# Two-layer transformer on one core: narrower causal-mask matmuls in the attention stage, router gates carried inside the dispatched rows, and a last stage that adds two rows

## The chip, the cores and the metric

The kernel runs on one core of one Trainium2 chip, as one program. The metric is the device time of one execution in microseconds (us), the median over the runs shown. Engines are named as in the profile: PE is the matmul engine (PEld its weight loads), DVE the vector engine, ACT the scalar engine, POOL the GpSimd engine, SP the engine that issues most DMAs.

## What is computed

The input is x[32, 256, 128] in float32: 32 batches of 256 tokens with 128 channels, 8192 tokens in all. Two layers follow each other, each an attention part and a mixture-of-experts part, both modulated per batch (`mod`). What matters here:

```
layer 0 attention (8 heads of 16):
  scores = (rope(q) . rope(k)) / 4;  scores = where(causal, scores, -inf)
  out    = softmax(scores) v, mixed with a second ("geometric") causal softmax; x = x + ga * out Wo
layer 0 experts (32, top 4); layer 1 attention (a delta rule over 256 steps), output projection
layer 1 experts (8, top 2):
  scores = rmsnorm(h) router;  ids = top2(scores);  c = softmax(scores)[ids]
  y_e    = W_down[e] (val * silu(gate)),  [val, gate] = W_up[e] rmsnorm(h)
  out    = sum over the 2 ids of c * y_id, plus h;  x = x + gb * out
```

## The kernel before

The kernel is a row of phases, each closed by a barrier over all engines: setup, load, attention, route, experts, project, delta, mix, ffn, combine. Inside a phase every engine has its own hand-written program, and they meet through semaphores. The change touches four phases; the order of the work in each is written out by hand.

**Attention** (`attention_phase`, from L467) loops over 32 batches, and over 2 groups of 4 heads in each. `scores` (L556 to L571) makes the scores of a group, for 8 blocks of 32 queries; a block's keys lie side by side in one of three PSUM banks (`KEYS_AT`: blocks 6 and 7 have 256 columns each in bank 0, blocks 4 and 5 have 192 and blocks 0 and 1 have 64 in bank 1, blocks 2 and 3 have 128 in bank 2). For each pair of blocks a bfloat16 matmul of the identity with a mask table (L565) first writes the causal term (-1e30 or 0) over all columns of both blocks; then one float32 product per block (L569, two records each in the profile) adds q.k on top. DVE reads the maxima bank by bank (`read_max`, L713), ACT makes the exponentials (L632), DVE transposes them (L725), and PE multiplies by the values (`weigh`, L581). PE's order in a batch is: scores of group 0, q and k of the next batch, scores of group 1, `front_geo`, weigh group 0, mix, weigh group 1, v of the next batch.

**Mix** (`mix_phase`, from L2236) goes through the tokens in 8 rounds of 1024. In each, the layer-1 attention output is projected, normalised and modulated, and the router picks 2 experts per token. DVE's `choose` finds them, `rank` gives each its place (L2696), ACT's `exps` makes exponentials (L2528), and DVE's `share` (L2700 to L2702) turns them into the two gates, written to the table `g.gate1`. POOL's `send` waits for the places, copies them (L2781), and issues 16 indirect DMAs (L2792), each of which scatters 128 rows of 132 floats (128 channels, then the row's destination number in column 128, then padding) to the area of the chosen expert; it then writes the next round's numbers (L2778). DVE's order in an iteration b is roots(b), choose(b-1), ..., rank(b-1), in the last one `tile_table` (L2710 to L2723), share(b-1), statistics, skip. In iteration b=1 choose and rank stand ahead of `scale_heads` (L2614), share behind it.

**Ffn** (`ffn_phase`, from L2801) takes 136 tiles of 128 rows: SP loads a tile (`xg`), PE multiplies with the expert's weights, DVE copies the result out of PSUM (L2942), and POOL scatters the rows by their number to `choice_rows`.

**Combine** (`combine_phase`, from L2955) goes through 16 chunks of 512 tokens, two to an iteration. SP loads the two rows of each token (two DMAs of 256 KB to a chunk, L2979, buffers for two chunks), DVE multiplies each by its gate (L3019) and adds them (L3025), PE transposes to channels (L2988), DVE applies the modulation and adds the kept x (L3031), PE transposes back (L2994), ACT copies out of PSUM (L3004) and issues the store (L3008). SP may load into a buffer again when its products have been taken.

## Time and profile before

| what | us |
|---|---|
| median of 3 runs (2347.59 to 2360.34) | 2350.3 |
| the profiled execution | 2352.5 |
| its span, first to last instruction | 2350.7 |
| PE / DVE / ACT / POOL busy | 1886.6 / 1631.3 / 1337.8 / 1241.9 |
| mean granted clock of PE | 0.869 of full speed |

The profile is one execution, so durations are those of that execution; 1.8 us lie outside its span. Share of busy time is an average over ten phases with different limits, so each phase is read by itself below.

### The profile page before, as it was taken

Reading aid. Unit: us, or ns where it says so; the run is one execution under the profiler, and the core shown is the slowest. Engines: PE = TensorE matmul, PEld = TensorE weight load, DVE = VectorE, ACT = ScalarE, POOL = GpSimd, SP = SyncE. Lnnn points to the kernel's source line nnn. Section 1 sums busy time; section 2 is a strip of 40 time slices with the busy share of each in tenths; the row PEclk is TensorE's granted clock in tenths of the full one; section 3 lists DMA queues with packets and bytes.
Section 4 is the critical chain, followed back from the end, with each engine's and each line's share of the span. In section 5 each row is a group of like instructions: output and inputs, shape, how many; then the busy total and the mean of one; then the engine's idle time right before and its main releaser. Section 6 shows DMA issues by size and latency. Waiting matters only on the chain. (4 is left out here: it accounts for less than half of the span.)

```text
span 2350.7 us, 38590 instructions
## 1 busy us (share of the span) xinstructions
PE 1886.6 (80%) x10634; PEld 1503.8 (64%) x10666; DVE 1631.3 (69%) x5209; ACT 1337.8 (57%) x3237; POOL 1241.9 (53%) x1241
## 2 busy tenths in 40 slices
PE   4689999999996663858996799999876641999975
PEld 3577777777774442325664688888765531999973
DVE  5678888888886695427996888888555442555547
ACT  3566666666663597316774688888444331555541
POOL 2177777777773000762324588888824454444430
PEclk8699999999998675978998899999876555999995
DMA  3000000000002112333200000000030011222217
GB/s 108 20 1 1 1 1 1 1 1 1 1 1 113 57 35 61 48 49 111 81 19 1 1 1 1 1 1 1 25 149 30 33 41 54 70 66 65 65 55 200
DMA packets 103522, 92.36 MB, mean 39 GB/s; under 512 B 11728, under 2 KB 93776, under 8 KB 102608
## 3 DMA queue, kind: packets, MB, share of 16 engines
q1 hardware_dynamic: 80272, 63.39, 8.7%
q0 software_dynamic: 14592, 22.30, 3.6%
q10 hardware_dynamic: 8448, 4.20, 0.6%
q8 instruction: 91, 1.49, 0.3%
q14 instruction: 119, 0.97, 0.1%
HBM read 46.87 MB, written 42.98 MB: 38 GB/s over the span
## 5 line engine op out<-in xcount | busy, mean ns | idle before, releaser
L581 PE MATMUL attn_out<-attn_turned,attn_v_diag 128*128 128x512 f32 (+7 forms) x1024 | 266.7, 414 | 22.4 <-DVE attn_turned L725 20.2
L618 ACT ACTIVATE attn_p_geo<-attn_kp_wide,attn_geo_cols 128x32 f32<-128x32 f32 (+6 forms) x448 | 179.6, 495 | 165.7 <-DVE attn_geo_cols L705 165.7
L581 PEld LDWEIGHTS attn_out<-attn_turned,attn_v_diag 128*128 128x128 f32 x1024 | 178.1, 191 | 122.3 <-issue 89.8
L2835 POOL DMA_INDIRECT choice_rows<-ffn_y,ffn_xg x136 | 130.9, 963 | 170.8 <-DVE ffn_y L2942 165.4
L2221 POOL TENSOR_TENSOR delta_A<-delta_A,delta_sW 128x256 f32<-128x256 f32 x256 | 186.9, 730 | 58.7 <-ACT delta_sW L2085 21.0
L569 PE MATMUL attn_score<-attn_k,attn_q_diag 128*128 128x256 f32 (+3 forms) x1024 | 183.5, 316 | 2.1 <-POOL attn_q_diag L797 0.5
L632 ACT ACTIVATE attn_p_att<-attn_score,attn_mx 128x224 f32<-128x224 f32 (+7 forms) x512 | 148.8, 390 | 62.4 <-DVE attn_mx L713 62.4
L2085 ACT ACTIVATE delta_sW<-delta_W,tables_sb 128x256 f32<-128x256 f32 x256 | 129.0, 506 | 79.2 <-DVE delta_W L2180 76.3
L569 PEld LDWEIGHTS attn_score<-attn_k,attn_q_diag 128*128 128x128 f32 x1024 | 157.5, 192 | 16.3
L2011 PE MATMUL delta_u<-delta_m,tables_sb 128*128 128x256 f32 x512 | 161.2, 397 | 3.6 <-DVE delta_m L2158 3.6
L2007 PE MATMUL delta_u<-delta_v_own,tables_sb 128*128 128x256 f32 x512 | 153.6, 382 | 8.7 <-DVE xnT L2145 8.7
L2019 PEld LDWEIGHTS delta_out<-delta_m,tables_sb 128*128 128x128 f32 x1024 | 131.9, 194 | 44.7 <-POOL delta_m L2232 40.9
L2019 PE MATMUL delta_out<-delta_m,tables_sb 128*128 128x128 f32 x1024 | 142.5, 283 | 19.9 <-POOL delta_m L2232 19.9
L2232 POOL TENSOR_TENSOR delta_m<-delta_A,delta_prod 128x1024 f32<-128x1024 f32 x64 | 151.4, 2365 | 5.0
L2792 POOL DMA_INDIRECT rows<-mix_rows,mix_slot x128 | 125.1, 978 | 44.9 <-issue 38.9
L2167 DVE TENSOR_TENSOR delta_u<-delta_u,delta_prod 128x256 f32<-128x256 f32 x256 | 110.8, 433 | 50.7 <-PE delta_u L2011 27.0
L713 DVE TENSOR_REDUCE attn_mx<-attn_score 128x2 f32<-128x512 f32 (+3 forms) x256 | 109.5, 478 | 43.4 <-PE attn_score L569 43.4
L1281 POOL DMA_INDIRECT exp_rows<-rows,slot_token x32 | 33.2, 1039 | 201.3 <-POOLq L136 191.8
L2180 DVE TENSOR_TENSOR delta_W<-delta_W,delta_u 128x128 f32<-128x128 f32 x512 | 133.7, 282 | 4.5
L797 POOL TENSOR_TENSOR attn_q_diag<-attn_q,tables_sb 128x1024 f32<-128x1024 f32 x64 | 120.4, 1905 | 0.0
L2934 DVE TENSOR_TENSOR ffn_hid<-ffn_sg,ffn_val 128x384 f32<-128x384 f32 x136 | 75.3, 554 | 61.6 <-PE ffn_val L2858 51.1
L725 DVE STREAM_TRANSPOSE attn_turned<-attn_p_att 128x32 f32<-128x32 f32 (+7 forms) x512 | 112.9, 288 | 2.7 <-ACT attn_p_att L632 2.7
(400 smaller groups left out, 5100.1 us busy)
## 6 DMA issues: line engine op xcount, KB each, us to landing
ffn_xg<-rows SPq DMA_DIRECT2D x136, 66.0 KB
acc<-route_zero SPq DMA_DIRECT2D x10, 832.0 KB
comb_rows<-choice_rows SPq DMA_DIRECT2D x32, 256.0 KB
rows<-route_rows SPq DMA_DIRECT2D x8, 640.0 KB, 3.5
load_rows<-in_x SPq DMA_DIRECT2D x16, 256.0 KB
bT<-acc SPq DMA_DIRECT2D x16, 256.0 KB, 3.9
qT<-acc SPq DMA_DIRECT2D x16, 256.0 KB, 4.6
x_kept<-xT SPq DMA_DIRECT2D x16, 256.0 KB, 2.1
```

The lines of the kernel that those rows point to most:

```text
L569: last = nc.tensor.matmul(score[bank][:, c:c + size], q_diag[:, gr, n], kk[:, par, 0:size], start=False, stop=n == here[-1])
L581: last = nc.tensor.matmul(out[:, :, SLOT * n:T], v_diag[:, gr, n], turned[:, :, gr, n * T + SLOT * n:(n + 1) * T], start=n == 0, stop=n == ...
L618: nc.scalar.activation(p_geo[:, gr, EARLY_OFF[n]:EARLY_OFF[n + 1]], kp_wide[:, par, gr, 0:n, :].rearrange("p n i -> p (n i)"), ACT.Exp, sc ...
L632: last = nc.scalar.activation(p_att[:, gr, ROW_OFF[n]:ROW_OFF[n + 1]], score[at][:, c:c + SLOT * (n + 1)], ACT.Exp, bias=mx[:, gr, n:n + 1])
L2007: nc.tensor.matmul(corrections(h, pp % 2), g.t("same_head"), moving, start=True, stop=False)
L2011: nc.tensor.matmul(corrections(h, pp % 2), g.t("same_head"), m1[:, h].rearrange("p t d b -> p (t d b)"), start=False, stop=True).then_inc( ...
L2019: last = nc.tensor.matmul(out_ps[parity][:, 0:QUAD * B], g.t(f"give{d}"), m3[:, parity, :, d, :], start=d == 0, stop=d == DH1 - 1)
L2085: nc.scalar.activation(sW[:, step % RING, :], W[:, step % RING].rearrange("p d b -> p (d b)"), ACT.Copy, scale=g.t("step")[:, bass.ds(step ...
L2180: nc.vector.tensor_tensor(W[:, t % RING, :, some(h)], W[:, (t - 1) % RING, :, some(h)], changes(h, pp % 2)[:, n], ALU.subtract).then_inc(b ...
L2221: nc.gpsimd.tensor_tensor(A[:, t % 8], A[:, (t - 1) % 8], sW[:, t % RING], ALU.add).then_inc(k.A, 1)
L2232: nc.gpsimd.tensor_tensor(m3[:, t // QUAD % 2], sums, query, ALU.mult).then_inc(k.m3, 1)
L2835: nc.gpsimd.indirect_dma_start(g.choice_rows, bass.IndirectOffsetOnAxis(xg[:, n % RING, D:D + 1].bitcast(U32), 0), y[:, n % RING, :], None ...
```

## The change

1. Attention: the mask matmul covers only the last 64 columns of each block, 128 columns in all, in place of 512, 384, 256 and 128. For blocks 4 and 6 (`TRIMMED`) the q.k product is cut to the 160 and 224 columns that a query of the block can see.
2. Gates: `share` writes the two gates of a token to column 129 of the rows to be sent. POOL's `send` therefore waits for the end of the round's route chain (`c.route`) before its first DMA. In iteration b=1 ACT's `exps` moves ahead of `add_bias` and `modulate`, and DVE's `share` ahead of `scale_heads`. In ffn, DVE's copy out of PSUM becomes a multiplication by the gate that came with the row.
3. Combine: the multiplications are gone; loads are four chunks deep, each chunk is a step of its own, and PE and DVE interleave chunk c with chunk c-1.

```diff
@@ -85,8 +85,8 @@
-    own, none = np.where(late, NEG, 0.0), np.zeros((128, T))
-    b["mask_pair"] = np.concatenate([none[:, 2 * SLOT:], own, none[:, SLOT:], own[:, 0:SLOT]], axis=1)
+    own, none = np.where(late, NEG, 0.0), np.zeros((128, SLOT))
+    b["mask_pair"] = np.concatenate([own, none, own[:, 0:SLOT]], axis=1)
...
+TRIMMED = (4, 6)
...
@@ -562,12 +563,14 @@
                     for n in here[1::2]:
                         _, c, size = KEYS_AT[n]
                         pair = score[bank][:, c - size:c + size].rearrange("p (n j) -> p n j", n=2)
-                        nc.tensor.matmul(pair, g.t("ident_bf"), g.t("mask_pair").rearrange("p (n j) -> p n j", n=2)[:, :, T - size:T],
-                                         start=n == here[1], stop=False)
+                        nc.tensor.matmul(pair[:, :, size - 2 * SLOT:size], g.t("ident_bf"),
+                                         g.t("mask_pair").rearrange("p (n j) -> p n j", n=2),
+                                         start=n == here[1], stop=False, skip_group_check=True)
                     for n in here:
                         _, c, size = KEYS_AT[n]
-                        last = nc.tensor.matmul(score[bank][:, c:c + size], q_diag[:, gr, n], kk[:, par, 0:size],
-                                                start=False, stop=n == here[-1])
+                        seen = SLOT * (n + 1) if n in TRIMMED else size
+                        last = nc.tensor.matmul(score[bank][:, c:c + seen], q_diag[:, gr, n], kk[:, par, 0:seen],
+                                                start=False, stop=n == here[-1], skip_group_check=True)
...
                 if b >= 1:
                     copy_rows(b - 1, 0)
+                if b == 1:
+                    exps(b - 1)
                 for par in both:
...
                 if b >= 1:
                     copy_rows(b - 1, 1)
+                if b > 1:
                     exps(b - 1)
...
@@ -2699,8 +2704,10 @@
                 dve.wait_ge(c.exp, i + 1)
...
-                then(nc.vector.tensor_tensor(g.gate1[:, tiles(i), :], ex[:, :, E1:E1 + K1], total[:, :, None].to_broadcast([128, SIDE, K1]),
-                                             ALU.mult))
+                shares = rows[:, i % 2, :, :, :, D + 1].rearrange("p a j n -> p (a j) n")
+                if i == 0:
+                    dve.wait_ge(c.ids_made, 3)
+                then(nc.vector.tensor_tensor(shares, ex[:, :, E1:E1 + K1], total[:, :, None].to_broadcast([128, SIDE, K1]), ALU.mult))
...
                 if b == 1:
                     then = choose(b - 1)
                     rank(b - 1)
+                    share(b - 1, then)
...
                 if b == LAST + 1:
                     tile_table()
-                if b >= 1:
+                if b > 1:
                     share(b - 1, then)
...
-            nc.gpsimd.memset(rows[:, :, :, :, :, D + 1:ROW1].rearrange("p a b j n w -> p (a b j n) w"), 0.0).then_inc(c.ids_made, 1)
+            nc.gpsimd.memset(rows[:, :, :, :, :, D + 2:ROW1].rearrange("p a b j n w -> p (a b j n) w"), 0.0).then_inc(c.ids_made, 1)
...
                 pool.wait_ge(c.named, i + 1)
                 pool.wait_ge(c.slots, i + 1)
+                pool.wait_ge(c.route, ROUTE * (i + 1))
                 for par in both:
                     pool.wait_ge(k[par].rows_read, i + 1)
...
                 dve.wait_ge(k[par].down, n // 2 + 1)
                 if n >= RING:
                     dve.wait_ge(ring[n % RING].sent, 16 * (n // RING))
-                nc.vector.tensor_copy(y[:, n % RING, :], y_ps[par][:, 0:D]).then_inc(k[par].y, 1)
+                nc.vector.tensor_scalar(y[:, n % RING, :], y_ps[par][:, 0:D], xg[:, n % RING, D + 1:D + 2], None, ALU.mult)\
+                    .then_inc(k[par].y, 1)
...
+    DEEP = 4
     with Scope(nc, "comb") as s:
-        rows = s.sb("rows", [128, PAR, K1, TILES, D])
-        part = s.sb("part", [128, PAR, K1, TILES, D])
-        mixed = s.sb("mixed", [128, PAR, TILES, D])
...
+            for c in range(NCH):
+                if c >= DEEP:
+                    sp.wait_ge(k.mixed, c - DEEP + 1)
+                for n in range(K1):
+                    sp.dma_start(rows[:, c % DEEP, n], by_tile(g.choice_rows[chunk(c, n * N), :])).then_inc(rows_in[c % DEEP], 16)
...
+            def turn(c):
+                pe.wait_ge(k.mixed, c + 1)
+                if c > 1:
+                    pe.wait_ge(k.y, c - 1)
+                for r in range(TILES):
+                    last = nc.tensor.transpose(by_channel[c % 2][:, 128 * r:128 * r + 128], mixed[:, c % 2, r, :], g.t("ident"))
+                last.then_inc(k.turned, 1)
+
+            def back(c):
+                pe.wait_ge(k.y, c + 1)
+                if c > 1:
+                    pe.wait_ge(k.copied, c - 1)
+                for r in range(TILES):
+                    last = nc.tensor.transpose(by_row[c % 2][:, 128 * r:128 * r + 128], y[:, c % 2, 128 * r:128 * r + 128],
+                                               g.t("ident"))
+                last.then_inc(k.back, 1)
+
+            for c in range(NCH + 1):
+                if c < NCH:
+                    turn(c)
+                if c > 0:
+                    back(c - 1)
...
+            def add(c):
+                dve.wait_ge(rows_in[c % DEEP], 32 * (c // DEEP + 1))
+                if c > 1:
+                    dve.wait_ge(k.turned, c - 1)
+                nc.vector.tensor_tensor(mixed[:, c % 2], rows[:, c % DEEP, 0], rows[:, c % DEEP, 1], ALU.add).then_inc(k.mixed, 1)
...
+            def gate(c):
+                dve.wait_ge(k.turned, c + 1)
...
+            for c in range(NCH + 1):
+                if c < NCH:
+                    add(c)
+                if c > 0:
+                    gate(c - 1)
...
-        g.gate1 = ctx.enter_context(nc.sbuf_tensor("gate1", tiles, F32))
```

## Rows read from the trace of the kernel before

**Rows 1.** timeline of one attention batch: start us, duration us, engine, line, what

```profile
409.38 4.18 PE L581 MATMUL attn_out<-attn_turned,attn_v_diag 128*128 128x512 f32 x16 [0.66 <-DVE attn_turned L725]
...
415.16 0.69 DVE L713 TENSOR_REDUCE attn_mx<-attn_score 128x2 f32<-128x512 f32 x1 [0.78 <-PE attn_score L569]
...
416.48 1.09 DVE L713 TENSOR_REDUCE attn_mx<-attn_score 128x2 f32<-128x384 f32 x3 [0.62 <-PE attn_score L569]
...
417.26 1.58 ACT L632 ACTIVATE attn_p_att<-attn_score,attn_mx 128x160 f32<-128x160 f32 x6 [0.46 <-DVE attn_mx L713]
```

**Rows 2.** page, part 5: busy us, mean ns, then idle us before

```profile
L713 DVE TENSOR_REDUCE attn_mx<-attn_score 128x2 f32<-128x512 f32 (+3 forms) x256 | 109.5, 478 | 43.4 <-PE attn_score L569 43.4
...
L725 DVE STREAM_TRANSPOSE attn_turned<-attn_p_att 128x32 f32<-128x32 f32 (+7 forms) x512 | 112.9, 288 | 2.7 <-ACT attn_p_att L632 2.7
```

**Rows 3.** timeline of POOL in mix: rounds 1 and 6, and the last round

```profile
1781.53 0.98 POOL L2792 DMA_INDIRECT rows<-mix_rows,mix_slot  x1 [0.77 <-POOL mix_slot L2781]
...
1801.80 0.22 POOL L2778 COPY mix_rows<-mix_ids 128x16 uint32<-128x16 uint32 x1
...
1932.42 0.98 POOL L2792 DMA_INDIRECT rows<-mix_rows,mix_slot  x1 [0.77 <-POOL mix_slot L2781]
...
1957.22 0.98 POOL L2792 DMA_INDIRECT rows<-mix_rows,mix_slot  x1 [0.77 <-POOL mix_slot L2781]
1960.40 1.79 POOL L2792 DMA_INDIRECT rows<-mix_rows,mix_slot  x1 [2.19 <-issue]
...
1978.93 0.96 POOL L2792 DMA_INDIRECT rows<-mix_rows,mix_slot  x1 [0.30 <-issue]
```

**Rows 4.** timeline of DVE over the same rounds, and ffn's first instruction

```profile
1782.82 0.20 DVE L2702 TENSOR_TENSOR gate<-mix_ex,mix_total 128x16 f32<-128x16 f32 x1
...
1804.41 1.29 DVE L2614 TENSOR_TENSOR mix_on<-mix_mid,xnT 128x512 f32<-128x512 f32 x2 [13.95 <-remote]
...
1934.55 0.18 DVE L2702 TENSOR_TENSOR gate<-mix_ex,mix_total 128x16 f32<-128x16 f32 x1
...
1963.53 0.17 DVE L2702 TENSOR_TENSOR gate<-mix_ex,mix_total 128x16 f32<-128x16 f32 x1
...
1984.22 0.27 DVE L2919 MEMSET ffn_w_up<- 128x256 f32 x1 [20.51 <-PEq L136]
```

**Rows 5.** stretches in us: busy us of each engine, PE's clock, DMA share, GB/s

```profile
2005.00:2275.00 270.00, 270.00 (x2423) 270.00 (x2422) 150.86 (x382) 159.56 (x380) 123.13 (x128) 1.00 0.23 63
2288.00:2340.00 52.00, 26.86 (x112) 20.37 (x112) 38.86 (x72) 7.99 (x14) 0.00 (x0) 0.53 0.79 222
2300.00:2306.00 6.00, 3.86 (x16) 3.00 (x16) 4.90 (x10) 0.60 (x1) 0.00 (x0) 0.50 0.93 259
2340.00:2350.70 10.70, 3.94 (x16) 3.01 (x16) 4.67 (x9) 1.57 (x3) 0.00 (x0) 0.50 0.32 99
```

**Rows 6.** timeline of PE on the mask and score products, group 1 of a batch

```profile
399.45 0.38 PE L565 MATMUL attn_score<-tables_bf_sb 128*128 128x512 bf16 x1
...
399.66 1.03 PE L569 MATMUL attn_score<-attn_k,attn_q_diag 128*128 128x256 f32 x4
...
400.53 0.38 PE L565 MATMUL attn_score<-tables_bf_sb 128*128 128x384 bf16 x2
...
400.74 1.26 PE L569 MATMUL attn_score<-attn_k,attn_q_diag 128*128 128x192 f32 x8
...
401.84 0.27 PE L565 MATMUL attn_score<-tables_bf_sb 128*128 128x256 bf16 x1
```

**Rows 7.** timeline of the end of combine

```profile
2341.66 1.29 DVE L3025 TENSOR_TENSOR comb_mixed<-comb_part 128x512 f32<-128x512 f32 x2
...
2342.40 1.97 PE L2988 MATMUL comb_by_channel<-tables_sb,comb_mixed 128*128 128x128 f32 x8 [2.66 <-DVE comb_mixed L3025]
2343.55 1.73 DVE L3031 SCALAR_TENSOR_TENSOR comb_y<-comb_by_channel,mod,xT 128x256 f32<-128x256 f32 x4 [0.61 <-PE comb_by_channel L2988]
...
2346.49 0.60 ACT L3004 ACTIVATE comb_done<-comb_by_row 128x512 f32<-128x512 f32 x1 [0.26 <-PE comb_by_row L2994]
```

More of the change, by code:

```diff
@@ L2569, in _ @@
             dve.wait_ge(c.consts, 5)
-            tiles = lambda i: bass.ds(i * SIDE, SIDE)
             def roots(run, heads, norm, rms):
@@ L2955, in combine_phase @@
 def combine_phase(nc, dram, g, out):
+    DEEP = 4
     with Scope(nc, "comb") as s:
-        rows = s.sb("rows", [128, PAR, K1, TILES, D])
-        part = s.sb("part", [128, PAR, K1, TILES, D])
-        mixed = s.sb("mixed", [128, PAR, TILES, D])
-        y = s.sb("y", [128, PAR, CH])
-        done = s.sb("done", [128, PAR, TILES, D])
-        by_channel = [s.ps(f"by_channel{par}") for par in range(PAR)]
-        by_row = [s.ps(f"by_row{par}") for par in range(PAR)]
-        k = [s.sems("in0 in1 part0 part1 mixed turned y back copied out", par) for par in range(PAR)]
+        rows = s.sb("rows", [128, DEEP, K1, TILES, D])
+        mixed = s.sb("mixed", [128, 2, TILES, D])
+        y = s.sb("y", [128, 2, CH])
+        done = s.sb("done", [128, DEEP, TILES, D])
+        by_channel = [s.ps(f"by_channel{n}") for n in range(2)]
+        by_row = [s.ps(f"by_row{n}") for n in range(2)]
+        k = s.sems("mixed turned y back copied")
+        rows_in = list(s.sems("in0 in1 in2 in3").values())
+        sent = list(s.sems("out0 out1 out2 out3").values())
         block = s.block()
         out_rows = out.rearrange("b t c -> (b t) c")
-        cols = lambda i, par, first=0: bass.ds(i * (PAR * CH) + par * CH + first, CH)
-        both = range(PAR)
+        chunk = lambda c, first=0: bass.ds(first + c * CH, CH)
         by_tile = lambda ap: ap.rearrange("(r p) c -> p r c", p=128)
@@ L2998, in _ @@
         @block.scalar
         def _(act):
-            for i in range(0, NCH // PAR):
-                for par in both:
-                    act.wait_ge(k[par].back, i + 1)
-                    act.wait_ge(k[par].out, 16 * i)
-                    nc.scalar.activation(done[:, par].rearrange("p r c -> p (r c)"), by_row[par][:, :], ACT.Copy)\
-                        .then_inc(k[par].copied, 1)
-                for par in both:
-                    act.wait_ge(k[par].copied, i + 1)
-                    act.dma_start(by_tile(out_rows[cols(i, par), :]), done[:, par]).then_inc(k[par].out, 16)
@@ L3009, in _ @@
-            for par in both:
-                act.wait_ge(k[par].out, 16 * (NCH // PAR))
+            for c in range(NCH):
+                act.wait_ge(k.back, c + 1)
+                if c >= DEEP:
+                    act.wait_ge(sent[c % DEEP], 16 * (c // DEEP))
+                nc.scalar.activation(done[:, c % DEEP].rearrange("p r c -> p (r c)"), by_row[c % 2][:, :], ACT.Copy).then_inc(k.copied, 1)
+                act.wait_ge(k.copied, c + 1)
+                act.dma_start(by_tile(out_rows[chunk(c), :]), done[:, c % DEEP]).then_inc(sent[c % DEEP], 16)
@@ L3012, in _ @@
+            for n in range(DEEP):
+                act.wait_ge(sent[n], 16 * (NCH // DEEP))
         @block.vector
         def _(dve):
-            for i in range(0, NCH // PAR):
-                for c in range(K1):
-                    for par in both:
-                        dve.wait_ge((k[par].in0, k[par].in1)[c], 16 * (i + 1))
-                        share = g.gate1[:, bass.ds(i * (PAR * TILES) + par * TILES, TILES), c:c + 1]
-                        nc.vector.tensor_tensor(part[:, par, c], rows[:, par, c], share.to_broadcast([128, TILES, D]), ALU.mult)\
-                            .then_inc((k[par].part0, k[par].part1)[c], 1)
-                for par in both:
-                    dve.wait_ge(k[par].part0, i + 1)
-                    dve.wait_ge(k[par].part1, i + 1)
-                    dve.wait_ge(k[par].turned, i)
-                    nc.vector.tensor_tensor(mixed[:, par], part[:, par, 0], part[:, par, 1], ALU.add).then_inc(k[par].mixed, 1)
-                for par in both:
-                    dve.wait_ge(k[par].turned, i + 1)
-                    dve.wait_ge(k[par].back, i)
-                    for j in range(BPC):
-                        b = i * (PAR * BPC) + par * BPC + j
-                        last = nc.vector.scalar_tensor_tensor(y[:, par, j * T:(j + 1) * T], by_channel[par][:, j * T:(j + 1) * T],
-                                                              g.mod[:, 1, 5, bass.ds(b, 1)], g.keptT[:, bass.ds(b * T, T)],
-                                                              ALU.mult, ALU.add)
-                    last.then_inc(k[par].y, 1)
@@ new lines, in add @@
+            def add(c):
[5 more added lines that the diff above has]
+                dve.wait_ge(k.turned, c + 1)
+                if c > 1:
+                    dve.wait_ge(k.back, c - 1)
+                for j in range(BPC):
+                    b = c * BPC + j
+                    last = nc.vector.scalar_tensor_tensor(y[:, c % 2, j * T:(j + 1) * T], by_channel[c % 2][:, j * T:(j + 1) * T],
+                                                          g.mod[:, 1, 5, bass.ds(b, 1)], g.keptT[:, bass.ds(b * T, T)],
+                                                          ALU.mult, ALU.add)
+                last.then_inc(k.y, 1)
@@ L3120, in build @@
         g.keptT = g.xT
-        tiles = (128, N // 128, K1)
-        g.gate1 = ctx.enter_context(nc.sbuf_tensor("gate1", tiles, F32))
         g.w_up = ctx.enter_context(nc.sbuf_tensor("w_up_sb", [128, E1 * 2, HID], F32))
```

20 lines of the change are left out of this document (removed).

## The prediction

> **What bounds the kernel now.** I read the page first: ten phases with different limits, so the 80% of PE says little, and the change touches four of them. Then came the stretches by phase, the timeline inside each, and the groups with their idle time.
>
> *Attention* is a loop through two engines. PE starts to weigh group 1 only when DVE has transposed it (idle 0.66 us), then makes v and the next batch's first scores; DVE meanwhile waits, 0.78 us for bank 0 and 0.62 us for bank 1 [rows 1]. Over all batches DVE waits 43.4 us for scores, 1.4 in each, while before the transposes it waits 2.7 us in all [rows 2]: behind the second bank DVE runs nearly dense round to the next weighing. So what PE saves between weighing and bank 1 of group 0 shortens the loop; what it saves in group 1 falls into its 0.66 us of idleness.
>
> *Mix* is set, unexpectedly, by POOL's sends. Round 1 issues its 16 from 1781.53 to 1801.80; DVE, which wants only a PE product for L2614, stands still 13.95 us and goes on at 1804.41 [rows 3, 4], 2.6 us behind the last send, though the trace puts that product's matmuls several us earlier. In all seven rounds that have a successor something in this chain resumes 2.5 to 2.9 us behind the last send. The page has no name for it ("remote"); I take it that PE's results are held up while the sends run. A later send is then a later round.
>
> *Ffn* is PE alone: 270.00 of 270 us busy [rows 5]. *Combine* waits for loads: with two chunks of buffers, a load starts when products are done. DMA engines are busy 0.79 of 2288 to 2340, 0.93 in a good stretch, 0.32 in the tail [rows 5].
>
> **Attention: the change on PE.** A float32 product of 256 columns takes 0.87 / 4 = 0.22 us per record, two passes of 0.107. One of 192 columns takes 0.163, so the four records of 64 columns in the row of eight take (1.10 - 0.65) / 4 = 0.11, not the 0.054 of their columns: 0.11 is the floor that the weight load sets [rows 6]. The 512-column mask takes 0.21; cut to 128 columns it would take 0.053, but the float32 weights behind it need 0.107, so bank 0 saves 0.107, and 2 x 0.027 for block 6 with 224 columns: 0.16. In bank 1 the 384-column mask falls from 0.16 to 0.053, since only another mask's light load follows; with 2 x 0.027 for block 4 that is 0.16 again. The masks of 256 and 128 columns already lie at or under the floor: nothing. On the path: 0.32 us in each of 31 later batches, **-9.9 us**. The same 0.32 in group 1 is hidden by PE's idleness. Next in line is ACT, with 0.46 us of idleness before its exponentials of banks 1 and 2 [rows 1]; 0.32 fits. The bounds are 0 (another wait takes over) and, if the floor did not hold, -12.
>
> Here a rule can be set against the row. The Trainium skill (TensorE: Matmul & The Clock Gate, Back-to-back issue gap) gives an isolated matmul a gap of its columns alone, and warns that this under-counts at few columns. By the columns alone bank 0 would save 0.21 and bank 1 0.16, 0.37 us a batch, 11.6 us in all. The records of 64 columns side with the warning, and the sum stays at 9.9.
>
> **Mix: the added wait.** POOL now waits for the gates before the first send; queued behind that wait are the 16 sends and the next round's numbers, and the next round, or ffn, waits for those. Between sends POOL idles 0.30 us [rows 3], so I take the first send 0.3 behind the gates' end. In round 1: 1782.82 + 0.20 + 0.3 = 1783.3 against 1781.53, 1.8 later. In round 6: 1934.73 + 0.3 against 1932.42, 2.6 later [rows 3, 4]. In the four between, the gates are ready between just before and 1.5 us after the first send; the six sum to 7.9. Round 0 has its exponentials and gates moved forward, with ACT's table load ahead of them; I put its send 0.6 us later. In the last round the tile table stands ahead of the gates: 1963.70 + 0.3 = 1964.0 against 1957.22, 6.8 later. But those 16 sends took until 1979.89, 22.7 us against the 20.3 of round 1, with a 2.19 us hole while DVE made the table [rows 3]; behind the table that hole closes, leaving about 4.0, and ffn's start moves with it [rows 4]. Sum if every delay counts: 0.6 + 7.9 + 4.0 = **+12.5 us**. The lower bound is +4, where only the last round counts; the upper +17, if the POOL launch takes the 0.77 us that it takes behind its own copy and round 0 loses the full 1.5 us by which its DVE work shifts. I take the sum, since every round resumes behind the sends.
>
> **Ffn and the rest.** DVE's copy becomes a multiplication by a per-row value over the same 128 x 128; there is no row for that form, so between the copy's own time and twice it. The cover is PE: DVE is busy 150.86 of 270 us [rows 5], and even 0.3 us more on each of 136 tiles leaves it below 200. Nothing. If the cover were gone, 41 us would lie open. The smaller mask table and the narrower memset lie in starts that wait for other work: nothing.
>
> **Combine.** The whole DMA work is 0.79 x 52 + 0.32 x 10.7 = 44.5 us at full share [rows 5]. Four chunks deep, loads need not wait for DVE: a chunk costs 2.8 us of DMA, while DVE needs 0.65 + 0.87 and PE 1.97 [rows 7]. SP issues two loads a chunk and ACT one store, all short against 2.8. The last three stores (2.8 us) still come behind the last load. At a share of 0.97, midway between the best stretch and 1, loads end at 2289 + 41.7 / 0.97 = 2332.0. The tail is an addition 0.65, transposes 1.0, modulation 0.9, transposes 1.0, four hand-overs of 0.1, and 4.2 from the last copy to the end (2346.49 to 2350.7): 8.2 [rows 7]. End 2340.2, **-10.5 us**. Bounds: -5.6 (share 0.93, no store left behind) and -12.
>
> **Sum.** -9.9 + 12.5 - 10.5 = -7.9. Against the profiled execution's 2352.5 that gives 2344.6; the median of the runs is 2.2 lower, so the forecast is 2342.4, 0.3% less than before. About 0.5%, 11.8 us, is what a measurement of this kernel can tell from no change.
>
> **Rivals.**
> - *The delays in mix are absorbed.* If what holds PE up ends by itself, or more of PE's chain slips through before the later sends, only the last round counts, +4. Against it: the constant 2.5 to 2.9 us. For it: the delay is 2 us in rounds of 25 to 36, and POOL has pauses. -9.9 + 4 - 10.5 = -16.4: 2333.9. Chance 0.27.
> - *Combine stays tied to DMA.* More loads and stores in flight may only lengthen each; share at 0.93 and no store left behind: -5.6 in place of -10.5, 2347.3. Chance 0.10.
> - *Narrow masks bring nothing*: the mask stays covered by the weight load or by ACT and POOL, whose slack is 0.46 us and less. Then the first part doesn't do what it says; 2352.3. Chance 0.09.
> - *Slower: fewer links slip through under the sends.* In rounds 5 and 6, 25 us long where rounds 1 to 4 have 32, only the count and the places are left behind the sends. If the later start costs these two that progress, each grows by 7: +14, 2356.3. It decides once the first matmul of `widen` is no longer done before the hold-up sets in; if rounds 1 to 4 also fall to the 36 us of round 0, up to 16 more. Chance 0.12.
>
> **Numbers.** The forecast has 0.42. 2330 to 2357 holds all but the far ends of the first rival (a floorless -12 in attention) and the heavy form of the last. Faster by over 0.5% (below 2338.5) is the absorbed case and a tail of the forecast, where combine and attention reach their far bounds: 0.36. Slower by over 0.5% is the heavy form of the last: 0.07. The rest, 0.57, is no change.
>
> **What would show it.** Right: DVE's idle time before L713 falls by about 10 us, attention by the same; sends begin 0.3 us behind the gates, rounds 1 and 6 start their successors 1.8 and 2.6 us later, ffn's first instruction stands at about 1984.2 - 9.9 + 12.5 = 1986.8; ffn lasts as long as before; combine takes some 52 us at a DMA share near 0.9. Wrong: a round that starts on time although its sends were late; a POOL launch that takes much more than 0.3 us behind the gates; PE idle in ffn with DVE as its releaser; DVE's wait for bank 1 gone, with ACT or POOL as the new releaser.

## The result, and the profile after

The changed kernel took 2325.49 us (median of 4 runs, 2325.06 to 2329.91) beside 2350.05 for the kernel before: a ratio of 0.9897, 95% interval 0.9877 to 0.9917, 24.6 us less. The forecast was 2342.4, in a range from 2330 to 2357. The profiled execution took 2325.7 us, with a span of 2323.9, which is 26.8 less than before. The trace gives the length of each stage, from its first instruction to that of the next:

| us | setup, load | attention | route | experts | project | delta | mix | ffn | combine |
|---|---|---|---|---|---|---|---|---|---|
| before | 109.9 | 634.8 | 187.8 | 120.4 | 223.4 | 421.4 | 285.7 | 303.6 | 62.9 |
| after | 111.1 | 625.5 | 183.7 | 126.2 | 224.5 | 421.5 | 283.0 | 303.1 | 44.5 |
| difference | +1.2 | -9.3 | -4.1 | +5.8 | +1.1 | +0.1 | -2.7 | -0.5 | -18.4 |
| forecast | 0 | -9.9 | 0 | 0 | 0 | 0 | +12.5 | 0 | -10.5 |

Route and experts, which the change leaves alone, come out at 183 to 184 or 188 to 193, and at 120 to 126, from run to run; their +1.7 together is no effect. So attention came as forecast, mix was 15.2 us better than forecast and combine 7.9.

**Attention.** The page of after, part 5 (busy us, mean ns, then idle us before; compare [rows 2]):

```profile
L716 DVE TENSOR_REDUCE attn_mx<-attn_score 128x2 f32<-128x512 f32 (+3 forms) x256 | 109.5, 478 | 33.6 <-PE attn_score L572 33.6
...
L728 DVE STREAM_TRANSPOSE attn_turned<-attn_p_att 128x32 f32<-128x32 f32 (+7 forms) x512 | 113.0, 289 | 2.7 <-ACT attn_p_att L635 2.7
```

DVE waits 9.8 us less for scores (43.4 before), the releaser is still PE, and the wait before the transposes, which would have grown if ACT had become the next limit, has stayed at 2.7. The timeline of PE over one group's scores (start, duration; compare [rows 6]):

```profile
396.32 0.22 PE L566 MATMUL attn_score<-tables_bf_sb 128*128 128x128 bf16 x1
396.38 1.03 PE L572 MATMUL attn_score<-attn_k,attn_q_diag 128*128 128x224 f32 x4
397.25 0.28 PE L566 MATMUL attn_score<-tables_bf_sb 128*128 128x128 bf16 x2
397.36 1.21 PE L572 MATMUL attn_score<-attn_k,attn_q_diag 128*128 128x160 f32 x8
```

From the mask of bank 0 to the first mask of bank 1 it is 0.93 us where it was 1.08, and from there to the mask of bank 2 (which starts at 398.40) 1.15 where it was 1.31: 0.15 and 0.16 less, as worked out.

**Mix.** The timeline of DVE and POOL in round 6 and where the last round begins (start, duration, idle before; compare [rows 3, 4]):

```profile
1926.25 0.23 DVE L2692 TENSOR_TENSOR mix_place<-mix_small,mix_base 128x64 f32<-128x64 f32 x1 [14.06 <-DMA exp_rows<-rows,slot_token]
...
1927.60 0.19 DVE L2710 TENSOR_TENSOR mix_rows<-mix_ex,mix_total 128x16 f32<-128x16 f32 x1
...
1944.02 0.19 DVE L2710 TENSOR_TENSOR mix_rows<-mix_ex,mix_total 128x16 f32<-128x16 f32 x1
```

```profile
1928.64 0.98 POOL L2801 DMA_INDIRECT rows<-mix_rows,mix_slot  x1 [1.18 <-issue]
...
1948.04 0.96 POOL L2801 DMA_INDIRECT rows<-mix_rows,mix_slot  x1 [0.30 <-issue]
...
1950.10 0.98 POOL L2801 DMA_INDIRECT rows<-mix_rows,mix_slot  x1 [0.77 <-issue]
```

Round 6 sends 0.85 us behind the end of its gates (1928.64 less 1927.79), not 0.3. The last round's gates stand ready at 1944.2, tile table included, while POOL is busy with the set of sends before until 1949.0: the new wait holds nothing there. Counted from the start of the stage, the first send of rounds 0 to 7 stands at

| | 0 | 1 | 2 | 3 | 4 | 5 | 6 | 7 | last send ends |
|---|---|---|---|---|---|---|---|---|---|
| before | 47.3 | 83.0 | 114.9 | 147.0 | 178.5 | 209.0 | 233.9 | 258.7 | 281.4 |
| after | 48.8 | 86.7 | 117.1 | 150.4 | 179.1 | 210.1 | 235.3 | 256.8 | 278.6 |

Rounds 0 and 1 are late by 1.5 and 3.7, more than I had priced (0.6 and 2.4); then the delay doesn't add up: it is 2.2, 3.4, 0.6, 1.1 and 1.4, and the last set starts 1.9 early.

**Combine.** Stretches of after (busy us of PE, PEld, DVE, ACT, POOL; PE's clock, DMA share, GB/s; compare [rows 5]):

```profile
2285.00:2291.00 6.00, 4.63 (x22) 3.88 (x22) 4.44 (x9) 1.19 (x2) 0.00 (x0) 0.51 1.17 292
2291.00:2297.00 6.00, 4.11 (x28) 2.68 (x27) 4.44 (x9) 1.79 (x3) 0.00 (x0) 1.00 1.16 328
...
2303.00:2309.00 6.00, 4.58 (x22) 3.40 (x20) 4.24 (x9) 1.79 (x3) 0.00 (x0) 0.58 1.15 345
...
2315.00:2323.90 8.90, 3.00 (x20) 1.81 (x18) 2.77 (x7) 1.79 (x3) 0.00 (x0) 0.87 0.54 167
```

The DMA engines are at 1.15 to 1.17, above the 1 that I took for a ceiling. The share adds up the time of packets, so a share above 1 says that packets of one engine overlapped. The packet work over the seven stretches from 2279 (four are shown; the shares of the six full ones add up to 6.52) is 6 x 6.52 + 8.9 x 0.54 = 43.9 us, close to the 44.5 of the forecast; it is done in less time.

### The profile page after: what moved, and what is told of

Same layout as the page of the kernel before. It is cut to its first block and busy times, and to the rows that moved or that the text cites. A ratio compares the mean times of both kernels' runs of the same rounds, so it can differ in the third digit from the quotient of the medians.

```text
span 2323.9 us, 38564 instructions
## 1 busy us (share of the span) xinstructions
PE 1881.0 (81%) x10666; PEld 1491.0 (64%) x10666; DVE 1618.6 (70%) x5177; ACT 1337.9 (58%) x3237; POOL 1241.1 (53%) x1241
## 5 line engine op out<-in xcount | busy, mean ns | idle before, releaser
L584 PE MATMUL attn_out<-attn_turned,attn_v_diag 128*128 128x512 f32 (+7 forms) x1024 | 268.8, 416 | 24.9 <-DVE attn_turned L728 21.4
L572 PE MATMUL attn_score<-attn_k,attn_q_diag 128*128 128x64 f32 (+5 forms) x1024 | 177.8, 317 | 0.0
L572 PEld LDWEIGHTS attn_score<-attn_k,attn_q_diag 128*128 128x128 f32 x1024 | 149.5, 193 | 7.3
L1284 POOL DMA_INDIRECT exp_rows<-rows,slot_token x32 | 33.6, 1049 | 197.5 <-POOLq L136 188.0
L716 DVE TENSOR_REDUCE attn_mx<-attn_score 128x2 f32<-128x512 f32 (+3 forms) x256 | 109.5, 478 | 33.6 <-PE attn_score L572 33.6
L800 POOL TENSOR_TENSOR attn_q_diag<-attn_q,tables_sb 128x1024 f32<-128x1024 f32 x64 | 120.4, 1903 | 0.2 <-PE attn_score L572 0.2
```

Of the source, the lines that this page charges most:

```text
L572: last = nc.tensor.matmul(score[bank][:, c:c + seen], q_diag[:, gr, n], kk[:, par, 0:seen], start=False, stop=n == here[-1], skip_group_ch ...
L584: last = nc.tensor.matmul(out[:, :, SLOT * n:T], v_diag[:, gr, n], turned[:, :, gr, n * T + SLOT * n:(n + 1) * T], start=n == 0, stop=n == ...
```

## The experiments

Times of different chips can't be compared (the kernel before took 2350 and 2347 us on two and 2300 to 2302 on four others), so every ratio is against the kernel before on the same chip, and stage lengths come from each run's own trace. The gap between those chips lies in mix. On the first two it lasts 275 to 291 us, because other engines stand still for long stretches while POOL sends ("the hold-up" below); on the other four it lasts 227 to 232. Of the kernel before, only one trace shows a chip with the hold-up, the one that the prediction was read from.

**One part at a time.** Four kernels, each the one before with one part of the change, on a chip without the hold-up. The edits are shown shortened.

The mask products and the trimmed columns:

```diff
-nc.tensor.matmul(pair, ..."mask_pair"...[:, :, T - size:T], ...)
+nc.tensor.matmul(pair[:, :, size - 2 * SLOT:size], ..."mask_pair"..., ...)
+seen = SLOT * (n + 1) if n in TRIMMED else size
```

> The kernel before with the attention part of the change alone (narrow masks, products of blocks 4 and 6 cut). Theory 'floor' (the step of the prediction): PE saves 0.32 us on the path in each of 31 batches, so the attention stage falls from 634.8 to about 625 us and the whole by 9.9 us (0.42%). Rival 'columns': 0.37 us a batch, 11.6 us. Rival 'nothing': another wait takes over, within 2 us of before. The mix stage has the same code as before (285.7 us); how far it moves here is what it moves by itself.

Measured: ratio 0.9949 (0.9931 to 0.9967), attention 624.9 us where the other kernels on this chip have 634.6 to 635.4, DVE's wait for scores 33.6. The ratio alone can't tell 9.9 us from 11.6; the stage and the wait side with 9.9. The price by the weight load's floor stands, and nothing else took over.

The wait, and round 0's exponentials and gates moved forward, the gates still in their table:

```diff
+pool.wait_ge(c.route, ROUTE * (i + 1))
...
+if b == 1: exps(b - 1)
...
+    share(b - 1, then)
```

> The kernel before with POOL's added wait for the gates and the forward move in round 0, gates still written to their table; nothing else. Theory 'held' (the prediction's): every round ends as much later as its sends begin later; with sends 0.86 us behind the gates, as in the changed kernel, that is about 12.5 + 4 = 16 us, mix 302 us, whole +0.7%. Rival 'absorbed': only the last round's sends count, +3 to +4 us, mix 289 us, whole +0.15%. Rival 'free': the rounds have other limits and the mix stage stays within 3 us of 285.7, as it does in the changed kernel (283.0).

Measured: ratio 0.9993 (0.9978 to 1.0008). But this chip has no hold-up: mix lasts 229.1, its rounds are POOL's own 21.4 us, and from round 2 on the gates are ready 4 to 15 us before POOL sends. Free here says nothing of the other kind of chip.

Combine four chunks deep with the multiplications kept, and the reverse, no multiplications (the gates in the rows, as in the change) in the old two-chunk combine:

```diff
-rows = s.sb("rows", [128, PAR, K1, TILES, D])
+rows = s.sb("rows", [128, DEEP, K1, TILES, D])
```

> The kernel before with the four-deep, chunk-by-chunk combine of the change, multiplications kept on DVE, gates in their table. Combine before: 62.9 us, in the changed kernel 44.5. If depth is what gave the 18.4 us: DVE then has 3 x 0.69 + 0.87 = 2.9 us a chunk, 47 us for 16, more than the DMA at 345 GB/s (2.3 us a chunk), so about 47 + 4 + 5 = 56 us, whole -7 us. If loads were limited to the share of 1.0 that the prediction took, no difference to that can be seen, since DVE is slower. If the multiplications never mattered: 45 us, -18 us.

```diff
-nc.vector.tensor_tensor(part[:, par, c], rows[:, par, c], share..., ALU.mult)   # 4 x an iteration
-nc.vector.tensor_tensor(mixed[:, par], part[:, par, 0], part[:, par, 1], ALU.add)
+nc.vector.tensor_tensor(mixed[:, par], rows[:, par, 0], rows[:, par, 1], ALU.add)
```

> The kernel before with the gates in the rows (mix and ffn as changed) and a combine of the old two-chunk structure whose multiplications are gone, a buffer being free once the addition is done. If the multiplications were on the loop of load and product: each of 8 iterations loses 2 x 0.65 us at least, combine about 62.9 - 10 = 52 us. If depth is everything: combine within 3 us of 62.9. Mix and ffn: theory 'held' wants mix at 302 us, 'absorbed' 289, 'free' 283 to 288; ffn stays at 303.5 in every theory.

Measured: combine 53.6 us, ratio 0.9959 (0.9942 to 0.9976), and 51.0 us, ratio 0.9953 (0.9933 to 0.9973). Against the 63 to 65 that combine takes as it was, depth with the chunk-by-chunk order gives some 10 and the missing products some 12.5; both together give 18.4, so some 4 are counted twice. Ffn with the multiplication in the copy's place took 304.4 us, within its spread (303.1 to 304.7).

**On a chip with the hold-up**: the changed kernel once more, the wait alone once more, and two other depths.

```diff
-DEEP = 4
+DEEP = 2   # f_deep2; DEEP sets the buffers of the loads and of the stores
+DEEP = 8   # f_deep8
```

> The changed kernel, measured again beside the parts. Additive theory: mask part -11.7, deep chunk-wise combine without multiplications -18.4, gates in the rows and the added wait 0 where mix runs at POOL's own pace (228 us): about -30 us, ratio 0.987. 'Held' theory: where mix takes 286 us in the kernel before, the added wait costs +12 to +16 and the ratio is 0.992 to 0.995.

> The kernel before with the added wait and the forward move in round 0 alone, once more. If mix takes 286 us in the kernel before on this chip, 'held' says +12 to +16 us, 'absorbed' +3 to +4, 'free' within 3. If mix takes 227 us, POOL alone sets the rounds (21.4 us each) and all say 0 to +2: round 0 begins its sends about 1 us behind the gates and nothing else is late.

> The changed kernel with loads two chunks deep in place of four. If depth lifts the DMA rate above what the prediction took as full: a load may start only when the addition two chunks back is done, DMA falls to about 250 GB/s, combine 44.5 to about 52 us, +0.3%. If the chunk-wise order and the shorter DVE work are enough: within 2 us of 44.5.

> The changed kernel with loads eight chunks deep. If combine now runs at the DMA engines' own rate (328 to 345 GB/s in its middle), no more depth helps: within 1 us of 44.5. If the rate still grows with what is in flight, combine falls by 2 to 4 us.

| | ratio (95%) | mix | combine |
|---|---|---|---|
| changed kernel | 0.9882 (0.9848 to 0.9917) | 278.5 | 44.9 |
| wait alone | 1.0009 (0.9989 to 1.0030) | 279.6 | 64.5 |
| depth 2 | 0.9898 (0.9874 to 0.9922) | 275.2 | 51.0 |
| depth 8 | 0.9864 (0.9836 to 0.9892) | 290.7 | 45.6 |

The wait alone costs nothing that can be measured, with the hold-up present (+2 us, interval -3 to +7): this is the run that takes my 12.5 us away. The wait was at work in it: in its trace the first sends of rounds 0 to 6 each stand 0.8 to 1.0 us behind their gates. Depth 4 is worth 6 us over depth 2, depth 8 no more; and at depth 2 the new order takes the same 51.0 us as the old order without products, so of the 18.4 us some 12 are the products and some 6 the depth, and the order alone gives nothing.

Mix moves from 275 to 291 between kernels that are the same there, so one trace on such a chip can't price a few us of it. In the one of 290.7 the last round's sends came 37.4 us behind those before, in the others 21.4 to 21.5. The timeline of POOL in that trace shows the last round's places taken and then a pause:

```profile
1941.91 0.20 POOL L2789 CAST mix_slot<-mix_place_of 128x16 uint32<-128x16 f32 x1 [8.79 <-DVE mix_place_of L2701]
1950.23 0.98 POOL L2801 DMA_INDIRECT rows<-mix_rows,mix_slot  x1 [8.12 <-issue]
```

DVE made the tile table from 1941.76 on and the gates behind it, until 1949.38. So the cost that I had put on the last round, a wait for gates behind the table, was paid in this one execution: 8.12 us of idle POOL where the launch behind its copies takes 0.77 [rows 3], some 7.3 us. In the four other traces with the wait on such a chip it was not.

**The attention term split**: the masks narrow, all score columns kept.

```diff
 last = nc.tensor.matmul(score[bank][:, c:c + size], ..., kk[:, par, 0:size], ...)
```

> The kernel before with the mask products cut to 128 columns, while the q.k products keep their full 192 and 256 columns. Of the 0.32 us a batch that the two edits gave together, my sum puts 0.107 + 0.107 on the narrow masks (a 512-column and a 384-column mask each fall to the float32 weight load behind them) and 0.054 + 0.054 on the trimmed columns. Theory (weight-load floor, both parts on the loop): attention 634.8 - 31 x 0.214 = 628.2, 6.6 us less, the rest of the 9.9 missing. Rival 1 (the masks pay by their columns and the trimmed columns lie under something): attention at 625, 9.9 us less. Rival 2 (the trimmed columns did most of it): attention at 631 or more.

Measured: ratio 0.9988 (0.9972 to 1.0003), attention 628.1. The page of this kernel, part 5, and below it that of the kernel before on the same chip:

```profile
L714 DVE TENSOR_REDUCE attn_mx<-attn_score 128x2 f32<-128x512 f32 (+3 forms) x256 | 109.4, 477 | 36.9 <-PE attn_score L570 36.9
```

```profile
L713 DVE TENSOR_REDUCE attn_mx<-attn_score 128x2 f32<-128x512 f32 (+3 forms) x256 | 109.4, 477 | 43.5 <-PE attn_score L569 43.5
```

The wait falls by 6.6 us = 31 x 0.214, to the tenth the two savings of 0.107 (one down to the floor, one of 256 columns); the other 3.3 (to 33.6) are the trimmed columns. By the mask's columns alone it would have been 0.16 + 0.107 a batch, 8.3 us. The ratio is little help: 6.6 us would be 0.9971, just outside its interval, and other stages differed from the trace beside it by as much (route by 5.2 us).

**The wait, doubled, and POOL paused.** The question left was why later sends cost nothing. All of these fell on chips without the hold-up (mix of the kernel before beside them 227.8, 227.5 and 231.7). A memset ahead of the first send of each round:

```diff
 pool.wait_ge(c.slots, i + 1)
+nc.gpsimd.memset(idle[:, :], 0.0)      # 128x2112
 for par in both:
```

> The kernel before with a POOL memset of 128x2112 in front of the first send of each round of mix, about 1.86 us each by the one row of that size, 15 us over eight rounds. It doubles the cost that I suspected: every run of sends starts 1.9 us later, with nothing else changed. On a chip with the hold-up (mix 280 to 286): my prediction's rule (a later run of sends is a later round) says mix 13 to 15 us longer; the rival (what is held gets through at other points, and a later run of sends is caught up) says less than 4 us. On a chip without it (mix 227, POOL-bound) both say 15 us longer, mix 242, and the run tells nothing on the rule.

> Again the kernel before with a POOL memset of 128x2112 (1.86 us each) in front of the first send of each round of mix. On a chip without the hold-up (mix 227 us) the first time gave 239.9, 12.4 us more. If this chip has the hold-up (mix about 280): my prediction's rule says mix 13 to 15 us longer than the kernel before beside it; the rival, that the delay is caught up, says less than 4 us. Without the hold-up: 240 again.

Measured: ratio 1.0034 (1.0017 to 1.0051), mix 239.9, 12.4 more for 14.9 us of memsets; then 1.0038 (1.0018 to 1.0057), mix 238.4, 6.7 more than the single trace beside it, which was itself 4 us longer than elsewhere. The ratios, over ten executions each, say 8 and 9 us more (4 to 13). Where POOL is the bound, some half or more of what is put on POOL is paid. On the rule, neither run tells anything.

A pause of 0.55 us after the first eight sends of a round:

```diff
                     nc.gpsimd.indirect_dma_start(...)
+                if par == 0:
+                    nc.gpsimd.memset(idle[:, :], 0.0)      # 128x512
```

> The kernel before with one POOL memset of 128x512 after the first 8 of the 16 sends of each round of mix, so that POOL's descriptor writing pauses once in the middle of a round. Nothing else changes. Theory A (where a round is held up, results of other engines are held until the whole run of sends is over): the last send is later by the memset, about 0.5 to 1.5 us, and so is each round: mix 4 to 12 us longer. Theory B (only descriptor writing holds them, and what is ready gets through at any pause): one link of the chain more passes in each round, and mix gets shorter by 2 us a round or more. On a chip without a hold-up, where mix lasts 227 us and is bound by POOL alone, both say: longer by 8 memsets.

Measured: 1.0026 (1.0006 to 1.0046), mix 231.0; repeated, 1.0008 (0.9992 to 1.0025), mix 232.9. Inconclusive for the same reason. The timeline of POOL in that kernel before beside it shows what such a chip does (start, duration, idle before): one set of sends ends, the copies follow, and the next set starts at once.

```profile
1788.06 0.96 POOL L2792 DMA_INDIRECT rows<-mix_rows,mix_slot  x1 [0.30 <-DMA rows<-mix_rows,mix_slot]
1789.02 0.23 POOL L2778 COPY mix_rows<-mix_ids 128x16 uint32<-128x16 uint32 x1
1789.16 0.20 POOL L2781 CAST mix_slot<-mix_place_of 128x16 uint32<-128x16 f32 x1
1790.13 0.97 POOL L2792 DMA_INDIRECT rows<-mix_rows,mix_slot  x1 [0.77 <-issue]
```

The last round's gates ahead of the tile table:

```diff
-if b == LAST + 1: tile_table()
 if b > 1: share(b - 1, then)
+if b == LAST + 1: tile_table()
```

> The changed kernel, with the gates of the last round of mix written ahead of the tile table in place of behind it. In its trace the last round's first send came 5.9 us after the gates, because POOL was still busy with the round before, so this order should bring nothing there: 0 us, mix as long as in the changed kernel on this chip. The rival is my prediction's term (the table stands in the way of the last round's sends): mix shorter by 4 us. With a depth of 8 in the last stage one trace showed the last sends only 0.86 us behind the gates; if that is a state that the kernel falls into, the rival can hold in some executions.

Measured: 0.9890 (0.9856 to 0.9923), mix 229.5; repeated, 0.9873 (0.9818 to 0.9928), mix 228.7, with the last gates ready 17 us before their sends. That is no gain beside the 228.9 of the kernel with the gates in the rows (the changed kernel itself has no trace on such a chip). The order was not seen on a chip with the hold-up, where the trace of depth 8 says that it could matter in some executions.

## Why the prediction was wrong

**Attention: right.** -9.9 forecast, -9.3 in the stage, -9.8 in DVE's wait, and masks and columns each confirmed apart. The rival "narrow masks bring nothing" falls. By columns alone it would have been 11.6. That is the rule of the Trainium skill (TensorE: Matmul & The Clock Gate, Back-to-back issue gap) for an isolated matmul, which the forecast set against the row; the traces (9.8 us, and 6.6 for the masks where columns give 8.3) side with that section's warning that it under-counts at few columns.

**Mix: wrong, by 15.2 us.** The step that failed is "A later send is then a later round" with its sum of 12.5. The wait alone, on a chip with the hold-up, came out at a ratio of 1.0009, where 12.5 us would be 1.0053, above the whole interval. The traces of before and after say where the sum went. It had 2.4 us up to the start of round 1, 6.1 in rounds 2 to 6 and 4.0 in the last. Measured are +3.7 up to the first send of round 1, -2.2 from there to the last send of round 6 (169.0 us, 171.2 before), and -4.2 from there to ffn (27.3, 31.5 before), together -2.7.

*Rounds 2 to 6.* The 2.5 to 2.9 us behind the last send were read rightly, and after the change some engine resumes so in six of the seven sets of sends. What was wrong is the step from there: it takes the same link of the chain to be the one that resumes. In before, L2614 makes both its products of round 1 behind the last send, after 13.95 us of stillness [rows 4]. The timeline of DVE and ACT after the change, with the sends from 1779.99 to 1799.98 (start, duration, idle before):

```profile
1784.82 0.28 ACT L2474 ACTIVATE mix_inv_t<-mix_mid 128x128 f32<-128x128 f32 x1 [4.01 <-issue]
...
1791.48 0.69 DVE L2619 TENSOR_TENSOR mix_on<-mix_mid,xnT 128x512 f32<-128x512 f32 x1 [4.78 <-remote]
...
1800.72 0.69 DVE L2619 TENSOR_TENSOR mix_on<-mix_mid,xnT 128x512 f32<-128x512 f32 x1 [8.55 <-remote]
...
1802.87 0.69 ACT L2493 ACTIVATE mix_mixed<-mix_mid,mix_per_channel 128x512 f32<-128x512 f32 x1 [11.77 <-remote]
```

The first product passed in the middle of the sends, the second stood until 0.7 us behind them, and what resumes 2.9 us behind the last send is ACT, a link further on. DVE's stillness is no shorter (4.78 + 8.55 = 13.3), but more of the chain lies behind it. In before the first of these links passed too, only later:

```profile
1793.03 0.28 ACT L2471 ACTIVATE mix_inv_t<-mix_mid 128x128 f32<-128x128 f32 x1 [8.34 <-DMA exp_rows<-rows,slot_token]
```

That is 11.5 us into the sends and 5.1 us behind the end of the PE product that it reads; after the change it is 4.8 us into them and right behind it. The table counts, of the last eight products on this line (L2614, and L2619 or L2617 in the changed kernels), those that start while POOL is inside a set of sends, and gives beside it the time from round 1's first send to the end of round 6's last:

| | before | after | changed, again | wait alone | depth 2 | depth 8 |
|---|---|---|---|---|---|---|
| products inside sends, of 8 | 2 | 4 | 6 | 6 | 8 | 5 |
| us | 171.2 | 169.0 | 167.2 | 166.2 | 163.0 | 161.1 |

In all five traces with the wait more of them pass under the sends than in the one without, and the rounds are shorter. That the later sends are the reason was not tested by itself, and of before there is only the one trace. DVE's groups over mix, in before, after, and before on a chip without the hold-up, show how much of the stage this line's wait is (busy, mean ns, then idle before):

```profile
L2614 DVE TENSOR_TENSOR mix_on<-mix_mid,xnT 128x512 f32<-128x512 f32 x12 | 7.9, 687 | 58.4 <-remote 58.1 <-issue 0.3
```

```profile
L2619 DVE TENSOR_TENSOR mix_on<-mix_mid,xnT 128x512 f32<-128x512 f32 x11 | 7.4, 689 | 48.5 <-remote 48.2 <-issue 0.3
```

```profile
L2614 DVE TENSOR_TENSOR mix_on<-mix_mid,xnT 128x512 f32<-128x512 f32 x11 | 7.3, 686 | 4.6 <-PE mix_mid L2368 4.3 <-issue 0.3
```

*The last round.* The 4.0 us for the tile table needed POOL to be idle when the gates came. In before, DVE's places for that round (L2687) came at 1955.24, 2.5 us behind the sends of round 6, and POOL waited for them. After the change they passed 6.8 us into those sends:

```profile
1935.43 0.23 DVE L2692 TENSOR_TENSOR mix_place<-mix_small,mix_base 128x64 f32<-128x64 f32 x1 [0.59 <-issue]
```

So table and gates were done while POOL was busy, and the last set began 1.1 us behind the one before it where it had been 4.5. Four of the five traces with the wait have this; in the fifth (depth 8) the places came behind the sends and the term was paid. The first rival, "delays absorbed", had the right mechanism, that more of the chain slips through before later sends, but kept the +4 of the last round, and so ended at 2333.9. It was given 0.27.

The launch behind the gates took 0.85 us, not 0.3. The 0.77 that the same instruction takes behind its copies [rows 3] was the nearer row, and I had used it only for the upper end; with it the failed sum would have come out higher still.

The slower rival ("fewer links slip through") falls: the period of round 5 stayed at 25 us, that of round 6 shrank from 24.8 to 21.5, and more links slipped through, not fewer.

**Ffn: right.** 303.1 us; the multiplication is covered.

**Combine: mechanism right, size wrong by 7.9 us.** The step is "at a share of 0.97, midway between the best stretch and 1". I read 0.93 and 259 GB/s from stretches of 6 us that had pauses in them [rows 5]. The DMA view of before in slices of 0.9 us, 2294 to 2330, had the answer (busy tenths, then GB/s):

```profile
DMA  0499940998999149889970799999897699932999
GB/s 0 125 336 288 278 129 15 286 271 204 340 294 295 50 135 290 213 262 344 307 199 2 222 266 195 346 267 307 232 271 228 171 339 275 297 98 69 282 214 293
DMA packets 16331, 8.13 MB, mean 226 GB/s; under 512 B 486, under 2 KB 16330, under 8 KB 16330
```

Bursts of 336 to 346, a mean of 226. The same view of after, 2285 to 2315:

```profile
DMA  9999999999999999999999999999999999999999
GB/s 296 299 291 290 290 290 291 292 288 294 339 344 330 339 343 348 345 346 345 364 326 332 344 348 343 346 345 344 348 346 343 346 312 320 344 344 333 346 344 333
DMA packets 19826, 9.86 MB, mean 329 GB/s; under 512 B 599, under 2 KB 19825, under 8 KB 19825
```

The burst rate has become the steady rate. Worked out from it, the transfers up to the last load (45 of the 48 of 256 KB, 11.8 MB; the forecast too left out the last three stores) take 11.8 / 0.329 = 35.9 us in place of the 43.0 of the forecast (41.7 / 0.97). Measured, the last load landed 37.3 us after the first was issued (2279.41 to 2316.7), the first 6 us at a lower rate of 209 GB/s. The forecast had 44.2 from the start of the stage, so this is 6.9 of the 7.9 us.

The Trainium skill (Perfetto Trace Analysis, Identifying the Most-Contended Engine) warns that the busy share of 16 DMA engines misleads, and to go by how much of the HBM bandwidth is used; a share of 1.17 in the trace agrees. The Trainium skill (DMA: Bandwidth & Descriptors, Specifications) gives an HBM limit of about 358 GB/s for a core, as half of what a stack gives two cores; by it the 11.8 MB would take 33.0 us, as an estimate. The trace, at 345 over 6 us and single slices of 348 (one of 364), comes close to that figure, but only one core ran here, and no run shows what set the 345.

The other 1.0 us is the tail, which was 7.2 us, not 8.2. The timeline of combine, its start and its end:

```profile
2286.43 1.12 PE L2998 MATMUL comb_by_channel<-tables_sb,comb_mixed 128*128 128x128 f32 x4 [1.37 <-DVE comb_mixed L3034]
...
2316.68 0.69 DVE L3034 TENSOR_TENSOR comb_mixed<-comb_rows 128x512 f32<-128x512 f32 x1 [1.23 <-DMA comb_rows<-choice_rows]
...
2317.43 0.66 PE L2998 MATMUL comb_by_channel<-tables_sb,comb_mixed 128*128 128x128 f32 x4 [1.26 <-DVE comb_mixed L3034]
...
2320.02 0.60 ACT L3022 ACTIVATE comb_done<-comb_by_row 128x512 f32<-128x512 f32 x1 [0.51 <-PE comb_by_row L3006]
```

Four transposes take 0.66 us here and 1.12 at the lower clock early in the stage (the granted clock is 0.87 over 2315 to 2323.9; the kernel before had 0.50 in its tail, the lower level of 1.2 GHz [rows 5]). The chain of waits of after, from 2279 to the end, names SP's own issuing of loads, with loads landing 5 to 7 us later:

```profile
by line: SPq L2989 51.7%; DMA comb_rows<-choice_rows 27.1%; issue 4.2%; ACT comb_done L3022 2.7%; DVE comb_y L3042 2.0%; DVE comb_mixed L3034 1.6%; PE comb_by_row L3006 1.5%; ACTq L3024 0.8%; DVEq L3039 0.0%; ACTq L3021 0.0%
...
2308.82 0.98 SPq L2989
2309.84 6.82 DMA comb_rows<-choice_rows
```

But an issue of SP is not the same length in both: in after the first six take 0.4 to 0.6 us and later ones mostly 0.7 to 1.5, in before nearly all take 0.36 to 0.55, and with depth 8 they are as long as in after, at the same 329 GB/s. So the issues lengthen when the transfers run at their full rate; 32 of 0.5 us would be 16 us. This speaks for the transfers, and not SP, as what ends the stage now; no run separated the two. "Combine stays tied to DMA" at 0.93 falls.

**Sum.** With the measured sizes the forecast's own frame gives -9.3 - 2.7 - 18.4 = -30.4; ffn with -0.5 and +4.1 from the stages that the change leaves (almost) alone make it the -26.8 of span. The error was in two terms, both of which made the forecast too slow: a cost that wasn't there and a gain taken too small.

**Open.** What holds the other engines up during POOL's sends on two of the chips was not settled; the runs meant for it fell on chips that don't show it. Nor is it known why a link passes under the sends in one execution and not in the next, which is what makes mix 275 us in one and 291 in another.

## What to carry to other kernels

Before a ceiling is set on transfers, read the trace of before in slices short enough that a burst stands alone: its peak, not the best average, is what deeper buffering reached here. A wait added in front of a queue costs only if that queue would have been idle, so look first at when it comes free; and even where it was idle and the sends did start later, as here in rounds 0 to 6, the rounds took no measurable time more. A regularity in when something resumes says nothing on what resumes: the 2.5 to 2.9 us were there before and after, but how much work had passed by then had changed. And a stage that differs by 50 us between chips needs its runs on the kind of chip where the question arises.

## What the runs showed of the hardware

- The same mix stage takes 275 to 291 us on two chips and 227 to 232 on four others, at the same 0.96 us for a send of POOL. In the kernel before, DVE stands still 58.4 us ahead of L2614 on one of the first kind, and 4.6 on one of the second.
- On the first kind a result can reach its reader late: ACT went on 5.1 us behind the PE product that it reads, in the middle of POOL's sends. Behind each of the seven sets of sends of before that have a successor some engine resumes 2.5 to 2.9 us after the last send; in the trace of depth 2 it is 1.2 us behind three of them.
- An issue of a 256 KB load on SP took 0.36 to 0.55 us in most cases at a mean of 226 GB/s, and 0.7 to 1.5 in most at 329.
- The DMA share can be 1.15 to 1.17 for 30 us, at up to 345 GB/s over 6 us, with loads and stores of 512-byte rows under way together.
- In combine PE's granted clock rose to 1.00 in two stretches of after (2291 to 2297, 4.11 us busy of 6, and 2309 to 2315, 3.68 busy), and was 0.51 and 0.58 in two others (2285 to 2291 and 2303 to 2309, 4.63 and 4.58 busy). The kernel before, 2.8 to 3.9 us busy in seven stretches of 6 us from 2294 to 2336, stayed at 0.50 in all but one (0.78).
